# Issuing the loads of q one slot later in an eight-stage transformer block, with one more pair sum on VectorE and the small variance steps on GpSimd

## What is computed

```
h = layernorm(x) * (1 + ca) + sa
x = x + ga * favor_attention(h)            # 16 heads, 64 random features, linear in T
h = layernorm(x) * (1 + cb) + sb
for e in range(4):                          # four quarters of 512 tokens, one per "expert"
    xn = layernorm(h[e]);  m = 256 >> e     # expert e uses the first m columns
    q[e], k[e], v[e] = (xn[:, :m] @ w[:, :m].T + bias for w in (q_w, k_w, v_w))
o = softmax(q @ k.T / 16) @ v               # 8 heads of width 32, over all 2048 tokens
x = x + gb * (h + padded projection of o[e][:, :m] for each e)
```

## Time and profile before

| | |
|---|---|
| median of three runs | 1766.48 us (1762.68 to 1766.83) |
| the profiled execution's own time | 1768.27 us |
| its span in the trace | 1766.5 us |
| PE busy | 1678.5 us, 95% of the span |
| VectorE, ACT, GpSimd busy | 1385.5, 1085.4, 1126.5 us (78%, 61%, 64%) |
| q1, SP's DMA queue | 54768 packets, 87.45 MB |

### The profile page before, as it was taken

The page is one execution under the profiler, slowest core; times in us unless marked ns, Lnnn a source line. Parts: engine busy times, 40 slices in busy tenths (PEclk is TensorE's granted clock), DMA queues, the critical chain, the costliest instruction groups (busy, mean ns, idle before and its releaser), DMA issues.

```text
span 1766.5 us, 32009 instructions
## 1 busy us (share of the span) xinstructions
PE 1678.5 (95%) x11538; PEld 970.8 (55%) x11538; DVE 1385.5 (78%) x2629; ACT 1085.4 (61%) x2066; POOL 1126.5 (64%) x1058
## 2 busy tenths in 40 slices
PE   6999989999999989999999998999999999899998
PEld 4776544444577554444467755444437765444443
DVE  5987978787688788787678878877858878787783
ACT  1885536566688553565668844466667875356665
POOL 2784358767678344867767734686686862477675
PEclk8999989999999998999999999999999999899999
DMA  6000360010200045001110005400120001520101
GB/s 188 2 1 1 103 188 15 19 46 25 73 2 1 1 152 143 10 19 46 58 40 2 2 16 174 106 19 10 46 72 25 2 1 58 179 61 18 39 17 48
DMA packets 56077, 89.57 MB, mean 51 GB/s; under 512 B 13288, under 2 KB 31976, under 8 KB 53100
## 3 DMA queue, kind: packets, MB, share of 16 engines
q1 hardware_dynamic: 54768, 87.45, 17.0%
q10 hardware_dynamic: 1152, 0.07, 0.0%
HBM read 49.29 MB, written 35.72 MB: 48 GB/s over the span
## 4 chain that ended last, share of the span: by engine, by line
PE 68%; DVE 16%; ACT 9%; DMA 2%; issue 2%; SPq 1%; POOL 1%; ACTq 0%; DVEq 0%; POOLq 0%
PE PS L1530 13%; PE PS L1705 12%; PE PS L1717 12%; PE PS L1730 6%; PE PS L1424 5%; DVE MXP L1111 4%; PE PS L1449 4%; PE PS L1432 3%; PE PS L1459 3%; ACT HT L670 2%; ACT HTR L673 2%; DVE STAT L1004 2%; ACT PR L901 2%; DVE QKS L1179 1%; ACT PHIQ L711 1%
## 5 line engine op out<-in xcount | busy, mean ns | idle before, releaser
L631 POOL TENSOR_TENSOR TS<-PR 128x1024 f32<-128x1024 f32 (+1 forms) x248 | 551.6, 2238 | 259.8 <-ACT PR L901 195.4
L1111 DVE TENSOR_REDUCE MXP<-PS 128x1 f32<-128x512 f32 x960 | 589.0, 681 | 145.9 <-PE PS L1530 145.2
L901 ACT ACTIVATE PR<-PS 128x512 f32<-128x512 f32 x960 | 487.6, 622 | 285.3 <-PE PS L1705 261.8
L1530 PE MATMUL PS<-KOP,QOP 96*128 96x512 f32 x960 | 406.8, 437 | 10.2 <-DVE MXP L1111 3.5
L1705 PE MATMUL PS<-QOP,KOP 97*128 97x512 f32 x960 | 376.5, 424 | 3.5 <-ACT QOP L888 3.1
L1530 PEld LDWEIGHTS PS<-KOP,QOP 96*128 96x128 f32 x960 | 186.2, 195 | 169.3 <-issue 90.4
L1705 PEld LDWEIGHTS PS<-QOP,KOP 97*128 97x128 f32 x960 | 180.3, 190 | 143.7 <-ACT PR L901 110.2
L1717 PE MATMUL PS<-PR,V 128*32 128x512 f32 x1920 | 255.1, 597 | 0.5
L1730 PE MATMUL PS<-TS,ones 128*32 128x512 f32 x960 | 136.0, 604 | 6.7 <-DVE TS L1289 6.7
L1717 PEld LDWEIGHTS PS<-PR,V 128*32 128x32 f32 x1920 | 62.2, 110 | 140.6 <-issue 98.4
L549 POOL TENSOR_SCALAR PK<-XSK 128x1024 f32<-128x1024 f32 x64 | 67.2, 1050 | 100.3 <-ACT XSK L733 100.3
(11 more groups left out here) (157 smaller groups left out, 2524.1 us busy)
## 6 DMA issues: line engine op xcount, KB each, us to landing
KOP<-k_scr SPq DMA_DIRECT2D x84, 256.0 KB, 5.7
k_scr<-QKS SPq DMA_DIRECT2D x64, 256.0 KB, 2.9
QOP<-q_scr SPq DMA_DIRECT2D x180, 64.0 KB, 2.0
q_scr<-QKS SPq DMA_DIRECT2D x40, 256.0 KB, 3.0
X<-in_L_attn_x_dram SPq DMA_DIRECT2D x16, 512.0 KB, 3.9
out_dram<-X SPq DMA_DIRECT2D x12, 512.0 KB, 3.0
QOP<-MXT SPq DMA_DIRECT2D x224, 0.5 KB
KOP<-QKS SPq DMA_DIRECT2D x36, 64.0 KB, 2.0
```

The costliest lines, as they stand in the source:

```text
L631: g.tensor_tensor(sums(k)[:, 0:len(stage)], pair[:, :, 0], pair[:, :, 1], ALU.add).then_inc(S["psum_t"], 1)
L901: a.activation(PR[:, k % 2, w, q], bank(score_bank(p, n, w, q)), ACT.Exp).then_inc(S["ex"], 1)
L1111: v.tensor_reduce(MXP[:, u % 2, i, kc:kc + 1], bank(max_bank(p)), AX.X, ALU.max).then_inc(S["am_rd"], 1)
L1530: mm(bank(max_bank(p)), QOP[0:96, u % QS6, i * P:(i + 1) * P], KOP[0:96, h % KS6, kc * CH:(kc + 1) * CH], start=True, stop=True).then_inc( ...
```

## The change

Three things are changed.

- SP's q loads of slot s are issued at the end of slot s + 1, behind the stores of its blocks, and no longer wait for the k block's store. Slot 0's own loads of KOP wait for block 0's store alone.
- VectorE no longer makes VE and NEGM for the second and third layernorm; GpSimd makes them, ahead of its power, with a wait of its own between.
- The pair sum of slot 62 goes from GpSimd to VectorE, so that VectorE makes the last three.

```diff
-        VECTOR_SUMS = (SLOTS - 3, SLOTS - 1)
+        VECTOR_SUMS = (SLOTS - 3, SLOTS - 2, SLOTS - 1)
...
+                def load_queries(s):
+                    wait_all(sp, *[stored(b, n) for n, t in blocks(s) if t >= 2])
+                    for u in range(QS6):
+                        if units[u][1] == expert[s]:
+                            load_q(b, u)
+
                 for s in range(NC):
...
-                    n0 = blocks(s)[0][0]
-                    wait_all(sp, stored(b, n0), stored(b, n0 + 2))
+                    if s > 0:
+                        load_queries(s - 1)
                     if s == 0:
+                        sp.wait_ge(*stored(b, 0))
...
-                    for u in range(QS6):
-                        if units[u][1] == e:
-                            load_q(b, u)
+                load_queries(NC - 1)
...
                 def deviations(s, h):
...
+                    g.tensor_scalar(VE[:, cols], MV[:, cols, 1], NORM_EPS, None, ALU.add).then_inc(S["ve2_e"], 1)
+                    wait_all(pool, (S["ve2_e"], n))
                     g.tensor_tensor(RSTD[:, cols], VE[:, cols], minus_half[:, cols], ALU.pow).then_inc(S["rstd2"], 1)
 
                 def deviations_again(s, h):
...
+                    g.tensor_scalar(VE[:, cols], MV[:, cols, 1], NORM_EPS, None, ALU.add).then_inc(S["ve3_e"], 1)
+                    g.tensor_scalar(NEGM[:, cols], MV[:, cols, 0], -1.0, None, ALU.mult).then_inc(S["negm"], 1)
+                    wait_all(pool, (S["ve3_e"], n))
...
-            def statistics(tiles, srcs, signal, negated=False):
+            def statistics(tiles, srcs, signal):
...
                 for t in tiles:
-                    v.bn_aggr(MV[:, t], STAT[:, t]).then_inc(S["dve_own"], 1)
-                    own.n += 1
-                dve.wait_ge(S["dve_own"], own.base + own.n)
-                sl = slice(tiles[0], tiles[-1] + 1)
-                if negated:
-                    v.tensor_scalar(NEGM[:, sl], MV[:, sl, 0], -1.0, None, ALU.mult).then_inc(S[signal], 1)
-                v.tensor_scalar(VE[:, sl], MV[:, sl, 1], NORM_EPS, None, ALU.add).then_inc(S[signal], 1)
+                    v.bn_aggr(MV[:, t], STAT[:, t]).then_inc(S[signal], 1)
...
                     if 2 * m == SLOTS - 2:
+                        pair_sum(b, SLOTS - 2)
                         pair_sum(b, SLOTS - 1)
```

More of the change, by code:

```diff
@@ L221, in adaln_block @@
                    den den_sb num num_sb denT rec rb rT mt yps x1
-                   ve2 rs3 rstd2 ve3 nmr3 h2 x2 x2T xn_sb qp q_hi q_lo scr0 scr1 scr2 vp v2_sb vb_ok obm
+                   ve2 ve2_e rs3 rstd2 ve3 ve3_e negm nmr3 h2 x2 x2T xn_sb qp q_hi q_lo scr0 scr1 scr2 vp v2_sb vb_ok obm
                    q_in0 q_in1 q_in2 q_in3 q_in4 q_in5 kf0 kf1 kf2 kf3 k_in1 k_in2 k_in3 k_in4 k_in5 k_in6 k_in7
@@ L570, in deviations @@
                     cols, n = halves(s, h), 2 * (NC * b + s) + h + 1
-                    wait_all(pool, (S["ve2"], n))
+                    wait_all(pool, (S["ve2"], 2 * n))
+                    g.tensor_scalar(VE[:, cols], MV[:, cols, 1], NORM_EPS, None, ALU.add).then_inc(S["ve2_e"], 1)
+                    wait_all(pool, (S["ve2_e"], n))
                     g.tensor_tensor(RSTD[:, cols], VE[:, cols], minus_half[:, cols], ALU.pow).then_inc(S["rstd2"], 1)
@@ L576, in deviations_again @@
                     wait_all(pool, (S["ve3"], 2 * n))
+                    g.tensor_scalar(VE[:, cols], MV[:, cols, 1], NORM_EPS, None, ALU.add).then_inc(S["ve3_e"], 1)
+                    g.tensor_scalar(NEGM[:, cols], MV[:, cols, 0], -1.0, None, ALU.mult).then_inc(S["negm"], 1)
+                    wait_all(pool, (S["ve3_e"], n))
                     g.tensor_tensor(RSTD[:, cols], VE[:, cols], minus_half[:, cols], ALU.pow).then_inc(S["rs3"], 1)
-                    wait_all(pool, (S["rs3"], n))
+                    wait_all(pool, (S["rs3"], n), (S["negm"], n))
                     g.tensor_tensor(NMR[:, cols], NEGM[:, cols], RSTD[:, cols], ALU.mult).then_inc(S["nmr3"], 1)
@@ L1173, in statistics_of_h @@
                     dve.wait_ge(S["h2"], TPC * (NC * b + s) + 2 * h + 2)
-                    statistics(halves(s, h), [Hh[:, t] for t in halves(s, h)], "ve3", negated=True)
+                    statistics(halves(s, h), [Hh[:, t] for t in halves(s, h)], "ve3")
                 def low_part(s, i):
```

## The result

| | before | changed kernel |
|---|---|---|
| median | 1766.48 us (1762.68 to 1767.30, 5 runs) | 1777.02 us (1774.78 to 1780.61, 5 runs) |
| the profiled execution's span | 1766.5 us | 1778.8 us (own time 1780.61) |
| PE, VectorE, GpSimd busy | 1678.5, 1385.5, 1126.5 us | 1677.0, 1372.3, 1140.6 us |

The ratio of the two kernels' times is 1.0058, 95% interval 1.0043 to 1.0074: slower by 10.2 us (7.6 to 13.1).

A forecast was written before the change was run, and what follows sets the result against it. Middle stage bound by PE and VectorE, then by waits through SP's queue; third stage by PE. Middle stage +16.8, third sum -4.6, together +12.2 on the median 1766.5: 1778.7 us, own range 1771 to 1787, 8-in-10 range 1765 to 1787.

The forecast's parts named there:

- Unit 0's load, moved: Middle stage: issued behind block 5's stores, unit 0's q load lands 5.9 us later per batch; PE waits for it.
- the earliest end: Middle stage: with the small steps off VectorE, block 5's low part ready at most 2.6 us early; 1.0 was taken.
- 0.61 us of PE's idle time: Middle stage: PE's slack in 36 us, said to cap what VectorE's lead from the small steps is worth.
- From Q to head 0's last operand: Middle stage, from PE's first maxima: 22.0 us without the clock's fall, 25.0 with it, where it was 26.3.
- The nine loads just hidden: Middle stage: SP's nine later q loads end 18.1 us after PE's first maxima; block 10 could be taken up at 18.0.
- The clock: Middle stage: PE idles some 7 us, then runs at granted clock 0.50; 3.0 us lost per batch, range 2.5 to 3.4.
- The rival of a second fall: Before head 0's last operand: PE waits 2 us, clock falls again, 1.5 us per batch; 1784.7 us, chance 0.10.
- The middle stage: Net loss from later unit 0's load, shorter way to head 0 and clock: +4.2 us per batch, +16.8 in four.
- The third sum: Batch end: slot 62's sum on VectorE ends slot 63's earlier, 1.4 us three times and 0.4 last, 4.6 gained.
- The two bounds built on 2.96 us as work: Batch end, durations read as work, not waiting: slot 63's sum 0.5 us earlier, or with 2.96 twice 0.9 later.
- The small steps: VE and NEGM moved from VectorE to GpSimd: block 5 ready 1.0 us earlier per batch; GpSimd's steps 0.2 us each.
- The rival of a clock that stays up: Middle stage: PE's clock doesn't fall at the new wait, 1.2 us lost per batch; 1766.7 us, no change, chance 0.15.

The follow-up runs named there:

- e1: Changed kernel with unit 0's three q loads back at the end of slot 0, only the nine loads of units 1, 2 and 5 later: 1743.16 us, ratio 0.9876.
- e7: Changed kernel plus eight matmuls that nobody reads on PE ahead of the wait for unit 0's load: 1766.31 us, ratio 1.0008.
- e5: Kernel before with only the nine q loads moved, and slot 0's KOP loads waiting for block 0's store alone: 1758.68 us, ratio 0.9966.
- e2: Kernel before with the new places of the q loads alone: 1795.86 us, ratio 1.0178.
- e3: Kernel before with slot 62's pair sum on VectorE and nothing else: 1758.51 us, ratio 0.9952.
- e4: Kernel before with the small variance steps on GpSimd and nothing else: 1762.19 us, ratio 0.9975.
- e10: Changed kernel with the small steps of the statistics on VectorE again: 1786.50 us, ratio 1.0122 to the kernel before.
- e8: Unit 0's q loads early and unit 1's behind slot 2's stores, as in e1, but units 2 and 5's behind block 10's loads and stores: 1737.39 us.
- e9: e8 plus one unread matmul behind each maximum of the third stage's first step while k is 0: 1733.06 us, ratio 0.9815 to the kernel before.

## Why the prediction was right

The sign and the mechanism of the loss came out as forecast: 12.2 us predicted, 10.2 measured by the ratios (7.6 to 13.1), 12.3 between the two profiled executions. That the sum is so close is luck in part. Tried alone, the loads cost 31.4 us where the forecast has 20.8 for them, and the sum and the small steps gain 8.5 and 4.4 where it has 4.6 and 4.0. That adds to +18.5, not +12.2, and the parts together gave +10.2, by an interplay that the forecast hadn't.

- **Unit 0's load, moved: right.** 5.9 us a batch predicted, 6.24 on average measured. Block 5's stores came 1.6 us earlier (M0 + 50.9 against 52.4), between the 1.0 that I took and the 2.6 that I had called the earliest end, and above the 0.61 us of PE's idle time that was to cap it. The three issues took 1.37 us instead of 1.23 and the landing 2.42 instead of 2.0, which used it up. e1 shows that without this wait there is no loss.
- **From Q to head 0's last operand: right.** 25.0 predicted with the clock's fall, 25.4 measured; 22.0 without it, 22.2 in e7. Block 9 could be taken up at Q + 13.5, not Q + 11.8, because the slow clock acts before it; ACT's wait there is 13.4 us in all and not nearly gone. From the first KOP load to block 9 it is 659.08 - 653.67 = 5.4 us, as it was before.
- **The nine loads just hidden: right.** They end at 665.60, Q + 20.1, and block 10's low part is written at 666.14, Q + 20.6; in the other three batches they end 0.1 to 0.9 us ahead of it too.

```profile
665.39 0.75 DVE L1183 SCALAR_TENSOR_TENSOR QKS<-PS,COLS,QKS 128x512 fp32r<-128x512 f32 x1 [1.25 <-ACT QKS L820]
```

e7, e5 and e1 show what "just" means: where PE is faster they end behind it, by 0.3 us in each batch of e7 and by up to 1.9 in e1. They are only a part of the waits for block 10's operands there: 1.0 of 9.2 us in e7, 2.9 of 9.1 in e5, 2.4 of 8.0 in e1.
- **The clock: right in its cost, incomplete in its places.** 3.0 us a batch was taken; e7 gives 3.2 between Q and K, 8.8 in the time. The first fall lasted 3.6 to 6.1 us behind PE's resuming, about 2.3 lost a batch, and a second one of 3.4 us was in every batch ahead of K. The two lose some 2.3 and 1.7 us of PE's work a batch, of which Q to K shows 3.2, so the second was nearly covered by the forecast's 3.0. The Trainium skill's rule ("TensorE: Matmul & The Clock Gate", "HAM oscillation — how this bites in real kernels"), that PE begins slow behind a wait for a DMA that is long enough, held for the four waits of 7.45 to 8.09 us.
- **The rival of a second fall** put one behind K. There is one there in each batch, but the kernel before has it as well (6.8 us each, here the second batch before and then after), so it isn't the new cost that the rival made of it. The 2 us of waiting ahead of K that it built on were 0.6 to 2.4.

```profile
675.00:681.00 6.00, 5.95 (x13) 3.16 (x14) 5.84 (x11) 1.19 (x2) 1.98 (x2) 0.50 0.48 149
```

```profile
684.00:690.00 6.00, 6.00 (x15) 2.27 (x16) 4.38 (x9) 1.19 (x2) 2.77 (x3) 0.50 0.96 231
```

- **The middle stage: under-sized.** +16.8 predicted, +19.3 in the changed kernel's trace. This forecast already held 1.0 us a batch for the small steps; without it the loads would be +20.8, and e2 measured +31.4. This is the largest miss. In e2's trace M0 to K has grown by 6.4 us a batch, 25.5 in all, 1.2 a batch more than I had: Q is 7.9 us later, not 6.9 (issue and landing took 0.5 more, and the batch that I took as the pattern had Q 0.25 late). The 5.9 us between 25.5 and 31.4 are mostly not in the two profiled executions, whose spans differ by 26.5: that of e2 is its fastest run, that of before one of its longer ones.
- **The third sum: right mechanism, under-sized.** 4.6 us predicted. Slot 63's sum took 2.96 us before and takes 1.22 now, so from the last exponential to D there are 1.40 us instead of 3.14: 1.7 three times and 0.3 in the last batch, 5.5 in all (I took 1.4 and 0.4). XH didn't hold back the sum, the sum held back XH (2.04 us instead of 1.23). D to the next M0 is shorter as well, by 3.4 us in all, 3.3 in e3. About 1.5 of these are the fall of the clock behind the first batch's 2.03-us wait, which I hadn't seen. Most of the rest goes with the other fall, ahead of M0: it lasts 14.8 us in three batches before, 10.3 in the changed kernel and 11.3 in e3, and nothing shows that the added sum shortens it. K to D shows only 3.7 of the 5.5 us, 4.2 in e3, so in e3's trace the two stages give 7.5 beside the 8.5 measured. The two bounds built on 2.96 us as work are refuted: 1.22 to 1.23 is the work.
- **The small steps: under-sized.** 4.0 us predicted through block 5, 4.4 alone (e4), 11 with the loads moved (e10), of which the traces place 5. GpSimd's new steps take 0.22 to 0.23 us in the median and 0.36 at most, where I took 0.2.
- **The rival of a clock that stays up** gave 1766.7; e7, where it does up to K, has 1766.31. Its sum was right and its premise wrong: PE's full stretch ahead of the wait didn't protect it.

## What to carry to other kernels

Before you move a load to a later place in an in-order DMA queue, ask for each unit of it when it is first needed and what stands behind that wait on the engine: here three DMAs of twelve were needed at once, and with the other nine moved their place made the difference between a gain of 22 us and a loss of 10. The best place for the rest can depend on it: the nine gained at their new place with the three early, and lost there with the three late, when at their old place SP had nothing else to do. A group of loads can be split, so that the urgent ones keep their place, and the ones with time go behind the next urgent issue. And a long idle time of PE can cost more than its length: in each of the four waits of 7.45 to 8.09 us the clock fell. Price both, and look for a fill before you accept the wait.

## What the runs showed of the hardware that I had not expected

- The same wait of 2.03 us on PE, ahead of the same instructions, was followed by a granted clock of 0.50 for about 3 us at 12 of 18 places and by 1.00 at the other 6. With a wait of 0.3 us there it fell at none of 21.
- PE was granted 0.50 also with no long wait: in e8 the longest idle time from 655 us on is 0.77 us, and the clock fell at about 661. Such a fall begins within 12.1 us behind K in every batch of the other twelve kernels, the one before among them. Unread matmuls between the maxima kept it at 1.00 in all four batches of e9.
- Both ways, VectorE's and GpSimd's instructions with both inputs in SBUF hold each other up. GpSimd's sum that began at 888.94 ended at 891.31, and VectorE's beside it at 892.40, 1.09 later, like the 1.08 that I had read from the earlier trace rows. GpSimd's power that followed took 1.55 us, median 0.56, and ended 0.41 behind VectorE's sum. The Trainium skill says that of the two it is the order of issue that decides which one blocks ("SBUF — State Buffer", "Who interferes with whom"), and the trace agrees both ways.
- The same nine DMA issues on SP took 4.03 us in each batch before and 4.17 to 4.18 in the changed kernel, but 4.17 to 4.19 in three batches of e1 and 5.80 in the fourth, and 4.17, 4.18, 5.23 and 5.81 in e5. Why they differ wasn't tried.
